# Ten middle batches of an unrolled attention layer, written as a hardware loop over pairs of batches

## What is computed

```python
q = x @ Wk.T + bk ; k = ctx @ Wk.T + bk ; v = ctx @ Wv.T + bv        # split into 16 heads
scores = q k^T / sqrt(32), causal mask
distcum = cumsum(softmax(scores)) ; disttotal = sum(softmax(scores))
dist = sqrt(clip((disttotal - distcum) * |i - j|, 0))
scores = scores * clip(exp(-softplus(gamma) * dist), 1e-5, 1e5)
out = softmax(scores, causal mask) @ v
x = layer_norm(x + out @ Wo.T + bo) * ln1_w + ln1_b
x = layer_norm(x + relu(x @ W1.T + b1) @ W2.T + b2) * ln2_w + ln2_b
```

## Time and profile before

| | |
|---|---|
| median of three runs | 1791.82 us |
| profiled execution, its own time | 1794.53 us |
| its span, first to last instruction | 1792.7 us |
| instructions in the span | 35252 |
| granted TensorE clock, mean | 0.932 of full speed |
| data moved | 334.18 MB |

### The profile page before, as it was taken

One profiled execution on the slowest core, in us unless ns is written; L12 is line 12 of the kernel. 1 busy time (PEld: TensorE's weight loads), 2 busy tenths in 40 slices (PEclk: granted clock), 3 DMA queues, 4 the chain that ended last, 5 costly groups with the idle time before them and its releaser, 6 DMA issues.

```text
span 1792.7 us, 35252 instructions
## 1 busy us (share of the span) xinstructions
PE 1548.0 (86%) x13056; PEld 1272.7 (71%) x13056; DVE 1130.3 (63%) x3828; ACT 1031.9 (58%) x2674; POOL 158.3 (9%) x107
## 2 busy tenths in 40 slices
PE   4474889898999999998989998998989899887775
PEld 3353578787877787886878787886878787666664
DVE  6676866767676776758676676757666666632221
ACT  1485765666666666666666566666666666642111
POOL 7322200101010000001010000001010000000000
PEclk9686989999999999999999999998999999899888
DMA  5544335556555555555555555655555554556654
GB/s 186 195 173 153 154 118 180 201 174 213 188 196 192 189 201 177 200 183 194 182 194 189 181 196 177 207 196 176 187 200 189 188 192 157 195 187 223 220 203 149
DMA packets 81210, 334.18 MB, mean 186 GB/s; under 512 B 10256, under 2 KB 10256, under 8 KB 64272
## 3 DMA queue, kind: packets, MB, share of 16 engines
q1 hardware_dynamic: 81040, 331.92, 54.5%
HBM read 306.72 MB, written 25.17 MB: 185 GB/s over the span
## 4 chain that ended last, share of the span: by engine, by line
PE 61%; DVE 16%; ACT 8%; DMA 6%; issue 6%; POOL 1%; SPq 1%; DVEq 0%; POOLq 0%; ACTq 0%
PE bank L200 18%; PE bank L201 16%; PE bank L202 16%; PE bank L369 5%; DVE w_sb L902 4%; DMA out<-rows 4%; DVE w_sb L914 4%; DVE h_lo L991 3%; PE bank L383 3%; ACT h_sb L704 2%; ACT h_hi L710 2%; ACT w_sb L632 1%; ACT w_sb L634 1%; DVE rows L979 1%; PE bank L403 1%
## 5 line engine op out<-in xcount | busy, mean ns | idle before, releaser
L991 DVE TENSOR_TENSOR h_lo<-h_sb,h_hi 128x512 fp32r<-128x512 f32 x128 | 107.3, 838 | 361.6 <-ACT h_hi L710 361.6
L200 PE MATMUL bank<-xt_hi,w_ring 128*128 128x256 f32 x1024 | 297.0, 290 | 12.1 <-issue 10.1
L200 PE MATMUL bank<-w_ring,h_hi 128*128 128x512 f32 x512 | 231.2, 452 | 83.6 <-DVE h_lo L991 83.6
L201 PE MATMUL bank<-xt_lo,w_ring 128*128 128x256 f32 x1024 | 289.0, 282 | 0.0
L202 PE MATMUL bank<-xt_hi,w_ring 128*128 128x256 f32 x1024 | 288.7, 282 | 0.0
L704 ACT ACTIVATE h_sb<-bank,b_col 128x256 f32<-128x256 f32 x256 | 106.4, 466 | 261.5 <-PE bank L202 261.5
L654 ACT COPY pt_sb<-bank 128x512 f32<-128x512 f32 x192 | 111.3, 580 | 186.9 <-PE bank L383 186.9
L201 PE MATMUL bank<-w_ring,h_hi 128*128 128x512 f32 x512 | 217.6, 425 | 0.0
L202 PE MATMUL bank<-w_ring,h_lo 128*128 128x512 f32 x512 | 217.0, 424 | 0.0
L200 PEld LDWEIGHTS bank<-xt_hi,w_ring 128*128 128x128 f32 x1024 | 195.1, 191 | 25.3 <-ACT xt_hi L693 16.2
L369 PE MATMUL bank<-qk_sb 32*32 32x256 f32 (+7 forms) x4096 | 176.8, 301 | 35.0 <-DVE m L890 34.7
(11 more groups left out here) (120 smaller groups left out, 3038.9 us busy)
## 6 DMA issues: line engine op xcount, KB each, us to landing
w_ring<-w_split SPq DMA_DIRECT2D x128, 1024.0 KB, 4.8
w_ring<-w_split SPq DMA_DIRECT2D x256, 512.0 KB, 3.4
w_split<-w_ring SPq DMA_DIRECT2D x32, 512.0 KB, 3.9
x_raw<-x_t SPq DMA_DIRECT2D x16, 512.0 KB, 5.3
c_raw<-ctx_t SPq DMA_DIRECT2D x16, 512.0 KB, 6.2
u_sb<-x_rows SPq DMA_DIRECT2D x16, 512.0 KB, 5.4
ring_raw<-w SPq DMA_DIRECT2D x32, 256.0 KB, 3.1
out<-rows SPq DMA_DIRECT2D x16, 512.0 KB, 6.0
```

The lines of the kernel that those rows point to most:

```text
L200: nc.tensor.matmul(dst, a_hi, b_hi, start=start, stop=False)
L201: nc.tensor.matmul(dst, a_hi, b_lo, start=False, stop=False)
L991: nc.vector.tensor_tensor(h_lo[:], h_sb[:], h_hi[:].bitcast(F32), ALU.subtract).then_inc(h_lo_ok, 1)
```

## The change

The steps i = 0 to 3 and 14 to 19 stay unrolled. The steps 4 to 13 are emitted as one loop body of two steps, which the engine runs five times with j = 2 to 6 in a register. `slot` is a constant in each half of the body (0 and 1), and every wait value and every DRAM address that has i in it becomes an expression of j.

```diff
             def plain(i):
                 step(i, i % 2, i < B, 1 <= i <= B, 2 <= i <= B + 1, 3 <= i <= B + 2, 4 <= i, i + 1 < B)
 
-            for i in range(B + 4):
+            for i in range(4):
+                plain(i)
+            with engine.Fori(2, B // 2 - 1) as j:
+                step(j * 2, 0, True, True, True, True, True, True)
+                step(j * 2 + 1, 1, True, True, True, True, True, True)
+            for i in range(B - 2, B + 4):
                 plain(i)
```

## The result

The changed kernel took 1813.97 us in the median of four runs (1810.75 to 1817.18, the profiled execution not among them), the kernel before 1791.27 us (four runs, 1783.26 to 1794.53). The ratio is 1.0134 (95% interval 1.0095 to 1.0172): 24 us slower, between 17 and 31. The profiled execution of the changed kernel took 1804.03 us with a span of 1801.9 us, shorter than the four others, so its span alone understates the loss. The ten looped steps show it clearly.

What follows compares the result with a forecast made beforehand. The prediction took PE to bound the looped steps, with about 61 us idle in ten; 1794.53 + 12 (values) + 4 (turns) = 1810.5 us, or 1808 us in terms of the median, range 1793 to 1832 us.

Steps and rivals of the forecast that it cites:

- the values: Wait values and addresses computed from j: 12 uncovered places a step at 0.10 us, 12 us in ten steps (0 to 24).
- the turns: Branches back at the loop's end, possible instruction misses: 1 us each (0 to 3.3), 4 us for four turns.
- The count of 356: Waits in a full step over all engines, each said to need at least one register operation; most cost nothing.
- Segment A: Stretch from PE's last matmul through SP's store and DVE to `add_hidden`, 15.8 us not set by PE; four value places.
- the low bound of the prediction: Values cost 0 us, as they may be made ahead of the wait that holds the engine.
- Fetches decide: Rival, 0.20: each turn costs PE 3.3 us plus 1.6 us of lower clock, 20 us; with 12 for values, 1824 us.
- Everything hidden: Rival, 0.16: values and misses are covered on all engines, no change, 1792 to 1795 us.
- Values cost twice: Rival, 0.12: two operations per value, dearer on PE; 24 us plus 4 us, 1820 us or more, to some 1832.
- faster: Rival, 0.07: a later store parts POOL's casts from DVE's L914, 7 us back in ten steps; 1788 us.
- Alternating distances: Sign that turns cost: of the distances between stores in the chain, every second one longer.
- Packets of q8: Sign in an instruction-load queue: near 105 if the body is loaded anew each pass, far fewer if it stays on chip.
- The signs of the values: Steps 4 to 13 each 1.2 us longer; PE's waits for `h_lo` and `pt_sb` up 8 to 12 us from 52.

Runs made afterwards that it cites:

- e5: The changed kernel with a branch hint on every engine at the head of each pass; ratio 0.9994 against the kernel before.
- e3: The changed kernel with only PE running the loop and ACT, DVE, SP and POOL unrolled; ratio 1.0128 against the kernel before.
- e11: The changed kernel with hints on all engines and SP's store issued ahead of the reloads of pairs 4 and 5; 0.9782 against the kernel before (1751 us).
- e8: The changed kernel with the branch hint on PE alone; ratio 0.9989 against the kernel before.

## Why the prediction came out as it did

**The direction and the total were right, the split was wrong.** The forecast was +16 us, of which 12 for the values and 4 for the turns. The measured +24 us are turns, but for at most 3 us. That the total came within 8 us is luck: one term was 9 to 12 us too large, the other 17 to 20 us too small.

**The values (12 places, 0.10 us each).** This step failed: the sum was 12 us and the runs leave 0 to 3 us. The count of 356 was too high, since the trace has 194 register operations a step, but the sum rests on the 12 places. Segment A's four can be read one by one. On DVE the value for `scaled1_ok` costs nothing: its last register operation (L981) starts at 1018.13, while the store is under way until 1023.02, so it is made ahead of the wait. The 0.09 us from the landing to DVE's start (1008.48 to 1008.57 in the earlier trace rows) are even less here, 0.03 us:

```profile
1017.31 5.71 DMA out<-rows
1023.02 0.03 issue
1023.05 1.41 DVE rows L984 x2
```

Two of the four lie on SP, between its reload and the store (compare), and there the values are on the way:

```profile
1016.64 0.32 SPq L263
...
1017.00 0.05 SPq L324
...
1017.17 0.04 SPq L326
...
1017.25 0.03 SPq L326
...
1017.31 5.71 DMA out<-rows
```

From 1016.64 to 1017.31 is 0.67 us, against 0.44 us before: three operations, 0.23 us, 0.08 us each, near the 0.10 us of the earlier trace rows. The fourth is PE's value for `w2_in`, and it is on the way as well. From the end of `h_lo` to `add_hidden` the kernel before takes 0.04 us, and the changed one 0.12 us, first and second fence (the same 0.12 us also stand in the changed kernel's segment A, at 1031.49):

```profile
1016.39 0.61 DVE h_lo L991
1017.00 0.04 issue
1017.05 0.50 PE bank L200
```

```profile
548.63 0.70 DVE h_lo L996
549.33 0.12 issue
549.45 0.49 PE bank L200
```

Over all of PE's waits for `h_lo` of more than 0.5 us in the ten steps the same step grows by 0.08 us or more, 0.10 us on average. So the price of one operation was right, and in three of segment A's four places it was paid. What did not come is the time at the end: e5, which has all these values, stands within 3 us of the kernel before, the low bound of the prediction. Its reason for that bound (the values are made ahead of the wait) holds on DVE and not on SP or PE. What takes the tenths back is not shown; the 410 semaphore instructions fewer, and the 0.06 us that DVE gains behind the store, are candidates.

**The turns (1 us each).** This step failed too, and by more: the size within its bounds, and the upper bound itself. The bounds of 0 and 3.3 us were worked out for one miss and for two misses. Both misses came. The first is somewhat dearer than its 1.1 to 3.1 us: the branch takes 3.5 us, the cover of 2.9 us hides most of it, and 0.9 us stick out where at most 0.2 us were expected. The second was taken for unlikely, and its cover was taken to be the same 2.9 us; it comes about 4 us after the first, with a cover of its own that depends on where the head lies. The clock's part, 1.9 us at the first turn, stood only in the rival (as 1.6 us). Measured: 0.93 + 2.98 + 1.86 = 5.8 us for the first turn in the trace, and 5.5 us on average by the distances of stores (105.8 against the 100.3 of the same steps before), where the forecast had 1 us.

**The rivals.** "Fetches decide" was the mechanism: 4 x 5 = 20 us foreseen, 21.4 us found in the ten steps of the profile. It had a chance of 0.20 where the forecast had 0.45. Its 12 us for values on top were not there, which is why it forecast 1824 and not 1812, and its argument that the engines' loads meet is answered by e3. "Everything hidden" is what the hinted loop shows, and what the change would have been with one more argument to `Fori`. "Values cost twice" and "faster" did not come; POOL's casts still lie beside DVE's scale operations (L914, here L919): 918.76 and 921.12 in the changed trace. The rule of the Trainium skill (Runtime: NRT & Kernel Launch, Instruction fetch mechanics), that a taken branch out of the loaded window makes execution wait for a fetch, agrees with the trace: 3.4 to 3.8 us on PE, 0.37 us with a hint. The figure of about 108 ns that the Trainium skill gives for a compare-and-branch (Advanced Engine Details and Errata, Control Flow Timing) is not met here: 40 to 68 ns on the other engines, 83 ns on PE where it falls through.

**The signs to look for.** Alternating distances and a wait at one place of every second step were named as signs of the fetch rival, and came. Packets of q8 "near 105" was loose: they are 117, three more for each turn. The signs of the values did not come: the steps without a turn are not 1.2 us longer but as long as before, and PE's waits for `h_lo` and `pt_sb` rose by 2 us and not by 8 to 12. The gap between SP's reload and the store grew by 0.23 us, as named; the one between a landing and DVE's start shrank.

## What to carry to other kernels

A loop with a body as long as this one costs at each turn on the engine that sets the time, here about 5.4 us of PE, and nothing on engines that wait there anyway; ask for the branch hint on the engine that sets the time, or at least put the head at the start of a block. Of the values computed from the loop's register, count only those made behind a wait, with work ready, above all addresses ahead of a transfer; here even these left at most 3 us at the end, and perhaps some 10 us once the store was early. And where the chain of waits goes through a store that an engine waits for, look at what the queue issues ahead of it: here the order of two lines was worth twice what the loop cost.

## What the runs showed of the hardware that I had not expected

After a turn two blocks are late, not one: the target's, with 3.5 us in the branch, and the next one, 3.7 to 4.5 us after PE resumes, at head positions with 8 and with 26 matmuls before the end of the block. A missing block is told in two ways: on PE in the record of the compare-and-branch (3464 ns in the median), on ACT as a gap of 2.97 us behind a branch of 45 ns. A branch hint seems to have a price once: after the last pass of the hinted loop ACT stood 3.6 us (e5) and 3.4 us (e11) for instructions, and without a hint on ACT (e8) it did not. And with one pass through a loop no register value is left (35267 instructions against 36811), so that such a kernel cannot serve to measure them.
